# A mixture-of-experts block: blank rows behind each expert instead of a fill of the sorted table, and a power made ahead of the first scatter

## The reference

```python
x = x + long_convolution(layernorm(x))        # projections, short filter, FFT filter, gate
x = x + experts(layernorm(x))
x = x + linear_attention(layernorm(x))        # 16 heads, causal
x = x + experts(layernorm(x))

def experts(x):                               # x is 4096 x 128
    logits = x @ gate_w                       # 8 experts
    top_val, top_id = max(logits), argmax(logits)
    xs = x * sigmoid(top_val)
    routed[t] = swiglu(xs[t], weights of expert top_id[t])   # 128 -> 256 -> 128
    return swiglu(x, shared weights) + routed
```

## Time and profile before

| | us |
|---|---|
| median of 3 runs | 540.97 (538.65 to 541.3) |
| profiled execution | 543.39 |
| its span in the trace | 541.7 |
| TensorE busy (matmuls) | 468.0 (86%) |
| VectorE busy | 368.3 (68%) |
| GpSimd busy | 342.9 (63%) |
| ScalarE busy | 260.7 (48%) |
| mean granted TensorE clock | 0.954 |

### The profile page before, as it was taken

How to read it: one execution, slowest core, us unless ns; L and a number is a source line. 1 busy time by engine, 2 the same in 40 slices (tenths; PEclk the granted TensorE clock), 3 DMA queues, 4 the chain that set the end, 5 groups by cost and what they waited for, 6 DMA issues and landing times.

```text
span 541.7 us, 14203 instructions
## 1 busy us (share of the span) xinstructions
PE 468.0 (86%) x4428; PEld 359.0 (66%) x4428; DVE 368.3 (68%) x1178; ACT 260.7 (48%) x671; POOL 342.9 (63%) x458
## 2 busy tenths in 40 slices
PE   3989999882999899993899999998686998999980
PEld 1668878771765799972566666666464665999960
DVE  6598999695776656643767778777475767666533
ACT  3553455023453355543776766766333452555530
POOL 4554676355886266661998888888566884466640
PEclk9999999998899999997999999999786999999995
DMA  8999999991111233315000000000000111333228
GB/s 277 323 225 185 190 177 189 185 163 35 45 46 46 66 88 90 92 48 160 2 2 2 3 2 2 4 1 3 1 12 31 41 45 51 84 86 91 79 74 271
DMA packets 49671, 47.66 MB, mean 88 GB/s; under 512 B 4186, under 2 KB 45019, under 8 KB 49470
## 3 DMA queue, kind: packets, MB, share of 16 engines
q1 hardware_dynamic: 44320, 35.90, 31.1%
q0 software_dynamic: 4544, 9.35, 5.1%
q10 hardware_dynamic: 734, 1.50, 0.8%
HBM read 17.86 MB, written 28.87 MB: 86 GB/s over the span
## 4 chain that ended last, share of the span: by engine, by line
PE 71%; DVE 7%; issue 6%; ACT 5%; POOL 5%; DMA 3%; SPq 1%; DVEq 0%; ACTq 0%; POOLq 0%
PE bank L781 65%; PE bank L297 2%; PE bank L861 2%; PE bank L791 1%; DMA scores_odd<-routed 1%; ACT scores_odd L1188 1%; DMA residual<-x 1%; ACT wide L1188 1%; DMA routed<-row_out,row_token 1%; ACT k_tok L1188 1%; POOL sorted_rows L648 1%; PE bank L1136 1%; POOL routed L660 1%; POOL spect_y L692 1%; DVE prod L1533 1%
## 5 line engine op out<-in xcount | busy, mean ns | idle before, releaser
L660 POOL DMA_INDIRECT routed<-row_out,row_token x78 | 74.7, 958 | 65.3 <-DVE row_token L1575 49.5
L781 PE MATMUL bank<-row_in_t,row_weights 128*128 128x128 f32 x624 | 83.7, 277 | 1.3 <-issue 1.0
L648 POOL DMA_INDIRECT sorted_rows<-rows,place x64 | 62.8, 981 | 25.7 <-issue 12.5
L781 PEld LDWEIGHTS bank<-row_in_t,row_weights 128*128 128x128 f32 x624 | 75.7, 191 | 3.0 <-issue 2.5
L781 PE MATMUL bank<-wide,weights_sb 128*128 128x512 f32 x128 | 60.7, 613 | 0.4 <-DVE residual L1813 0.4
L1567 DVE TENSOR_SCALAR row_weights<-experts 128x512 f32 x78 | 34.0, 436 | 27.6 <-issue 24.0
L1232 ACT ACTIVATE row_silu<-bank 128x256 f32<-128x256 f32 x78 | 29.9, 384 | 47.0 <-PE bank L781 45.8
L1188 ACT ACTIVATE wide<-bank 128x512 f32<-128x512 f32 x56 | 30.6, 593 | 44.9 <-PE bank L791 28.3
L781 PE MATMUL bank<-experts,row_act 128*128 x312 | 49.4, 282 | 0.0
L1559 DVE TENSOR_TENSOR row_act<-row_silu,bank 128x256 f32<-128x256 f32 x78 | 32.7, 420 | 20.1 <-ACT row_silu L1232 11.3
L781 PE MATMUL bank<-normed_t,weights_sb 128*128 128x256 f32 (+1 forms) x112 | 41.4, 500 | 0.9 <-ACT normed_t L1188 0.9
(11 more groups left out here) (184 smaller groups left out, 1067.7 us busy)
## 6 DMA issues: line engine op xcount, KB each, us to landing
sorted_rows<-zeros SPq DMA_DIRECT2D x1, 17028.0 KB, 101.2
row_in<-sorted_rows SPq DMA_DIRECT2D x78, 64.5 KB, 1.9
rows<-routed SPq DMA_DIRECT2D x8, 256.0 KB, 4.9
scores_odd<-routed SPq DMA_DIRECT2D x8, 256.0 KB, 5.8
out<-residual SPq DMA_DIRECT2D x8, 256.0 KB, 4.6
routed<-row_out,row_token POOLq DMA_INDIRECT x78
tables_sb<-tables SPq DMA_DIRECT2D x1, 1024.0 KB, 9.1
experts<-rt_gate SPq DMA_DIRECT2D x1, 1024.0 KB, 18.7
```

The source lines that it names most:

```text
L648: pool.indirect_dma_start(sorted_rows, bass.IndirectOffsetOnAxis(ap=place[:, t:t + 1].bitcast(U32), axis=0), rows[:, t, :], None).then_inc ...
L660: pool.indirect_dma_start(routed, bass.IndirectOffsetOnAxis(ap=row_token[:, r:r + 1].bitcast(U32), axis=0), row_out[:, r, :], None).then_i ...
L781: return pe.matmul(out_, lhsT, rhs, start=start, stop=stop, **kw)
```

## The change

The fill goes. In its place, in each of the two expert layers, SyncE writes blank rows behind each expert's last token: 128 rows for each of the first seven experts, and 1024 (LAST_BLANK = 8 tiles) for the last. Where they start is a new step of VectorE's table, made from the counts right behind `n_tok`; SyncE reads each start into a register. A new wait stands in front of the row loads, for all eight blanks. For this the regions grow by a tile each. The numbers of places carry an offset (FIRST) that is added at the cast of `place`, so that the counts stay exact in bf16. GpSimd's first scatters move from `second_exp` to behind the power of pair 2, and so also behind the root of pair 7; they no longer wait for a fill.

```diff
-REGION = TILES * P
-SORTED = -(-((E - 1) * REGION + RT * P) // (8 * P)) * 8 * P
-BLANK_N = 2 * (D + 1)
+REGION = (TILES + 1) * P
+FIRST = (E - 1) * P
+LAST_BLANK = E
+SORTED = (E - 1) * REGION + (TILES + LAST_BLANK) * P
+ROW = D + 1
+BLANK_N = 2 * ROW
...
-    c["region_share"] = np.tile(REGION // P * np.arange(E), (P, 1)) * 1.0
-    c["region_start"] = np.tile(REGION * np.arange(E), (P, 1)) * 1.0
+    c["region_share"] = np.tile((REGION * np.arange(E) - FIRST) // P, (P, 1)) * 1.0
+    c["region_start"] = np.tile(REGION * np.arange(E) - FIRST, (P, 1)) * 1.0
...
-        def clear_sorted(sp):
-
-            flat = sorted_rows.rearrange("r d -> (r d)").rearrange("(p n c) -> p n c", p=P, c=BLANK_N)
-            sp.dma_start(flat, zeros.unsqueeze(1).to_broadcast([P, SORTED // (2 * P), BLANK_N])
-                         ).then_inc(sorted_cleared, 16)
+        def blank_ends(sp, m):
+
+            sp.wait_ge(e_tiles, tabled_to("blank_start", m))
+            for e in range(E):
+                tiles = LAST_BLANK if e == E - 1 else 1
+                start = sp.value_load(blank_start[0:1, e:e + 1], min_val=0, max_val=SORTED - tiles * P)
+                behind = sorted_rows[bass.ds(start, tiles * P), :]
+                if tiles > 1:
+                    behind = behind.rearrange("(p a r) d -> p a (r d)", p=P, r=2)
+                    sp.dma_start(behind, zeros.unsqueeze(1).to_broadcast([P, tiles // 2, BLANK_N])).then_inc(blanked, 16)
+                else:
+                    sp.dma_start(behind, zeros[:, 0:ROW]).then_inc(blanked, 16)
...
         def routed_io(sp, m):
+            blank_ends(sp, m)
             sp.wait_ge(e_tiles, tabled_to("tile_base", m))
             sp.wait_ge(e_sent, 16 * TILES * (m + 1))
+            sp.wait_ge(blanked, 16 * E * (m + 1))
...
             sp.wait_ge(const_made, CONSTS)
-            clear_sorted(sp)
             routed_io(sp, 0)
...
                 if k == 0 and m == 0:
-                    pool.wait_ge(sorted_cleared, 16)
                     pool.wait_ge(tokens_numbered, 1)
...
             def second_exp():
                 exp_minus_top(1)
-                send_rows(0)
...
             exp_minus_top(2)
+            send_rows(0)
             send_rows(1)
...
-                routed_step("place", k, dve.tensor_copy(place[:, k * PAIR:(k + 1) * PAIR], place_f[:]))
+                routed_step("place", k, dve.tensor_scalar(place[:, k * PAIR:(k + 1) * PAIR], place_f[:], float(FIRST), None,
+                                                          ALU.add))
...
+                tabled_step("blank_start", dve.tensor_scalar(blank_start[:], rank_bank[m][:, PE_TILES:PE_TILES + E],
+                                                             float(FIRST), None, ALU.add))
```

More of the change, by code:

```diff
@@ L151, in hybrid_block @@
         bank = [ctx.enter_context(nc.psum_tensor(f"bank{i}", [P, 512], F32)) for i in range(8)]
-        sorted_rows = nc.dram_tensor("sorted_rows", [SORTED, D + 1], F32, kind="Internal").ap()
+        sorted_rows = nc.dram_tensor("sorted_rows", [SORTED, ROW], F32, kind="Internal").ap()
         routed = nc.dram_tensor("routed", [NO_TOKEN + RING * P, D], F32, kind="Internal").ap()
@@ L206, in hybrid_block @@
         normed_t = sb("normed_t", [P, PT])
-        rows = sb("rows", [P, TILES, D + 1])
+        rows = sb("rows", [P, TILES, ROW])
         wide = sb("wide", [P, TILES * D])
@@ L223, in hybrid_block @@
         const_made = sem("const_made")
-        sorted_cleared = sem("sorted_cleared")
+        blanked = sem("blanked")
         tokens_numbered = sem("tokens_numbered")
@@ L358, in hybrid_block @@
         n_tiles = sb("n_tiles", [P, E])
+        blank_start = sb("blank_start", [P, E], I32)
         tile_ends = sb("tile_ends", [P, E])
@@ L395, in down_bank @@
             return later_down_bank if shared_is_later(m, k) else down_banks[m]
-        row_in = sb("row_in", [P, RING, D + 1])
+        row_in = sb("row_in", [P, RING, ROW])
         row_token = sb("row_token", [P, RING], I32)
@@ L426, in hybrid_block @@
         ROUTE = ("top", "is_top", "ranked_top", "best", "chosen", "chosen_b", "so_far", "place_of", "place_f", "place")
-        TILE_TABLE = ("n_tok", "tiles_x", "tiles_round", "n_tiles", "tile_ends", "past", "expert_f", "tile_expert",
+        TILE_TABLE = ("n_tok", "blank_start", "tiles_x", "tiles_round", "n_tiles", "tile_ends", "past", "expert_f", "tile_expert",
                       "base_step", "base_of", "base_f", "base", "tile_base",
@@ L623, in _ @@
             sp.wait_ge(stored, 16 * PAIRS)
-            sp.wait_ge(sorted_cleared, 16)
             sp.wait_ge(loaded_experts, 16 * len(expert_loads))
```

## The result

| | before | after |
|---|---|---|
| median of the runs side by side | 539.81 (538.57 to 541.3, 4 runs) | 552.12 (551.46 to 552.69, 4 runs) |
| ratio | | 1.0226, 95% interval 1.0189 to 1.0264 |
| profiled execution, its span | 543.39, 541.7 | 552.69, 551.0 |
| mean granted TensorE clock | 0.954 | 0.940 |

The change costs 12.3 us, and the forecast was +6.0 with a range up to 551.5. The direction was right; the forecast size was about half of it, and the result lies outside the range.

A forecast was written before the change was run, and what follows sets the result against it. TensorE carried 71% of the chain, with a weak stretch where GpSimd's first scatter waited for the fill. First layer -0.4 + 1.5 and second +3.4 + 1.5 gave +6.0 us on 540.97: 547.0, range 541.5 to 551.5.

The forecast's parts named there:

- the offset: Whole kernel: the profiled execution before lies 2.4 us above the median, so 549.4 profiled was stated as 547.0.
- The one wait left is for the clear: GpSimd's first scatter, idle 5.68 us to 125.83, waits only for the sorted table's fill, landing at about 125.
- Part 1, the order: GpSimd's gating: no fill, pair 2's power before the scatters; row tiles would start 2.0 us sooner.
- the -0.4 of the first layer: First layer's tile 1: turned at 179.7 instead of 180.07, so 0.4 us gained before the clock's cost.
- Part 2, the pitch: SyncE's eight blank issues a layer: 1.1 us apart, the eighth starting 8.7 us after the table.
- Part 2, the landing of the large blank: Last blank's store before the row loads: 3.2 to 4.4 us, taken as 3.2, about 1.6 of it fixed.
- Part 3, the clock: TensorE at half clock after idling before the row tiles: 0 to 2.1 us a layer, taken as 1.5 each.
- Second layer by itself: Second expert layer: tiles start 3.4 us later behind the blanks, plus 1.5 us for the slower clock.
- The steady clock: TensorE before the row tiles: blanks gate but the clock stays up, +3.0 us, 544.0; chance 0.20.
- the blanks in time: SyncE's second-layer wait: last blank lands by 455.9, leaving only the 2.0 us gain, 539.0; chance 0.10.
- The harm of the clear's traffic: Convolution stage: fill traffic slows compute, removal gives 3 to 5 us more; about 543, or 536 without blanks' cost; chance 0.10.
- The blanks cost more: Large store at 4.4 us or beyond, held up by scatters on the same engines: +1.2 us per layer, 550 to 553; chance 0.15.

The follow-up runs named there:

- The issues without the wait: Kernel before plus SyncE issuing all sixteen blanks into a table nobody reads, nothing waiting for them before the end; 545.9 us, ratio 1.0103.
- the clock kept: Changed kernel with six unread 128x512 matmul products on TensorE in front of each layer's row tiles; 549.43 us, ratio 1.0194.
- the longer pieces: Kernel before with the same fill bytes in pieces of 4128 bytes in place of 1032; 540.37 us, ratio 1.0008.
- second execution of before: Kernel before run once more, unchanged, for a second profile; 540.17 us, ratio 1.0005.
- large blank first: Changed kernel with the last expert's large blank issued first and the small ones behind it; 551.6 us, ratio 1.0212.

## Why the prediction was wrong, step by step

The error of 6.3 us has two halves. The profiled execution was to take 549.4 and took 552.69: 3.3 us are costs of the blanks sized too low. The other 3.0 come from the reference: the profiled execution of before lies 3.6 us above its median (543.39 against 539.81), that of after 0.6 above its own (552.69 against 552.12). The late landing of the fill was in the first and can't be in the second, and I carried the offset over as if both had it. The traces bear this out: from pair 1's power to the first down matmul it is 64.0 us in the first profile of before and 59.4 to 59.7 in the three others whose first layer has the old order and no blanks, so the late fill cost that execution some 4.4 us. By layers: 6.3 measured for the second, so about 12.3 - 6.3 = 6.0 for the first; I had 4.9 and 1.1.

- **"The one wait left is for the clear" (what bounds the kernel).** True of the profiled execution and wrong for the kernel. In four other executions the fill landed 8 to 10 us sooner, and with the old order the first scatter then stands 0.33 us behind the power. That the profiled execution lay 2.4 us above the median (3.6 with the fourth execution) could have warned me; I used it only as an offset.
- **Part 1, the order, a gain of 2.0 us at the gate.** The positions came out (first scatter 126.46 for 126.5, last one's end 172.3 for 171.9, TensorE at 130.36 for 130.4), but against the wrong reference. Where the fill is in time, the move makes a saturated GpSimd idle for 3.8 us, and alone it costs 4.2 us in place of gaining 2.0. In the changed kernel the wait for the blanks covers that loss but for the 0.9 to 1.4 us by which the token count comes later, and the medians do not show those (552.4 with the old order, 552.12 with the new). So the -0.4 of the first layer set a gain against the blanks' cost that a typical execution does not have. My own place for tile 1's turn, 179.7, is 60.6 us behind pair 1's power. In the late execution that is 0.4 sooner than before (60.9), in the three clean ones (56.3 to 56.6) it would have been 4.0 to 4.3 later. This is the step that failed most, and the only one with the wrong sign.
- **Part 2, the pitch.** Taken 1.1 us, 7.7 for seven; the eighth blank started 8.5 and 7.9 us behind the first. Nearly right, 0.8 and 0.2 too low. Most of the 0.8 is that profile's own: in three other kernels with these blanks in this order it is 7.8 to 7.9 in the first layer.
- **Part 2, the landing of the large blank.** Taken 3.2 us, bounds 3.2 to 4.4; measured 4.8, above both ends. The bulk of the bytes was about as quick as I took it, 1.6 to 1.7 us. The fixed share was not 1.6 but 3.0: 1.2 us from the issue to the first packets and, in the second layer, 1.8 from the last packet to the end of the wait. In the first layer the tail of packets took 0.8 and what follows it 1.1. My fixed share came from a row load, a write into the core's own memory, and from the scatters. By the rule of the Trainium skill that I set beside it (DMA: Bandwidth & Descriptors, Anatomy of one DMA), which the page fits to DMAs issued by GpSimd while this store is SyncE's, the estimate was 3.2 too; the trace does not agree, its number is 4.8. The Trainium skill also warns that the semaphore's update waits for the write to be confirmed and that this can be long where the target is HBM (Perfetto Trace Analysis, DMA Instruction — HWDGE). The 1.8 and 1.1 us behind the last packets agree with that; no run here shows what passes in them. Mis-sized by 1.6 us a layer: the first row load went out at 178.85 where I had said 176.7.
- **Part 2, loads behind the store.** I counted no cost for what the blanks do to the row loads. The issues without the wait show one: 3.9 us from the first row load's issue to its turn in place of 1.9. In the changed kernel the wait covers it.
- **Part 3, the clock.** Taken 1.5 us a layer, 3.0 in all. Measured with the clock kept: 2.7 us (549.43 against 552.12, with 2 to 3 us of uncertainty). Right in sum, as far as that tells; in the profiled execution it was 2.4 and about 1.5.
- **Second layer by itself.** Forecast +3.4 + 1.5 = 4.9; measured +6.3. The difference of 1.4 is about the landing's 1.6, which the interval of that run (3.5 to 8.9) allows but can't prove; in the changed kernel's own profile the second layer is dearer by 22.0 - 16.0 = 6.0. Twice 6.3 is 12.6, against 12.3 for the change.
- **The rivals.** The steady clock and the blanks in time fell. The harm of the clear's traffic fell outright (windows above, and the longer pieces). "The blanks cost more" (550 to 553, 0.15) was the case that came, for the reason it gave, the landing, though not by scatters on the same engines: with the large blank issued last, behind the scatters, or first, among them, it landed in 4.6 to 5.0 us. That the number fits is half luck: 3.0 us of the way came from the reference, which that rival did not have.

Open: why the fill landed in 101 us in one execution and in 91 to 93 in four (it was slower all the way, 186 GB/s from 45 to 110 us against 203 in the second execution of before, and not held up at one place); and how the 6.4 us that come only with the wait split between the landing and what TensorE does with it, since large blank first moved the row loads by 1.7 (0.8 of it that profile's own) and 0.8 us and the median by 0.5.

## What to carry to other kernels

A wait seen in one profiled execution is a property of that execution until a second one shows it, above all where it hangs on a long transfer landing near its deadline; and then the gain of any step that fills that wait must be priced with the wait and without it. Work in the background that nobody waits for (here 17 MB of zeros beside the convolution) can cost nothing, while an eighteenth of it a layer (0.99 MB) on the path costs 6 us: eight issues on a queue, a landing, a late load and a half clock behind them.

## What was not expected of the hardware

- A store of 516 KB to HBM took 4.6 to 5.0 us from issue to landing in every kernel, about 1.7 of it packets (in the second layer of the changed kernel), with 1.2 in front of the first and 1.8 behind the last; one of 64.5 KB took 1.9 to 3.6, as medians of the kernels.
- The fill ran at 186 GB/s in pieces of 1032 bytes (203 in another execution) and at 405 GB/s in pieces of 4128. Neither slowed an engine: pair 1's power stands at 119.14 and 119.23, and at 119.10 without a fill.
- The landing of the same fill varied from 91 to 101 us between executions, with the same instructions beside it; the kernel before alone had 101.2 and 92.0.
